# One copy of the weighting loop in the second cross attention: mask products under a condition, sums cleared first, first mask taken among the queries

## The reference, cut to what matters

```python
# first layer: keys and queries normalised per head; a padding mask over the 8192 keys
attn = jnp.where(padding_mask[:, None, None, :], attn, -jnp.inf)
# second layer
scores = jnp.einsum('bhqd,bhkd->bhqk', Q, K) / jnp.sqrt(jnp.float32(D))
scores = jnp.where(mask == 1, jnp.float32(-1000000000.0), scores)   # (1, 1, 512, 8192)
attn = jax.nn.softmax(scores, axis=-1)
out = jnp.einsum('bhqk,bhkd->bhqd', attn, V)
return out.transpose(0, 2, 1, 3).reshape(Bq, Sq, E) @ Wo.T + bo
```

## Time and profile before

| | us |
|---|---|
| median of 3 runs | 1766.46 |
| the 3 runs | 1765.86 to 1768.48 |
| the profiled execution, its own time | 1768.05 |
| its span, first to last instruction | 1766.3 |
| L0x, from the start to the end of its denominators | 0 to 463 |
| self attention and mixture of the first layer | to 985 |
| L1x, first half | 985 to 1209 |
| L1x, second half up to the inverse of the denominators | 1209 to 1411 |

### The profile page before, as it was taken

One profiled execution on the slowest core, in us unless ns is written; L12 is line 12 of the kernel. 1 busy time (PEld: TensorE's weight loads), 2 busy tenths in 40 slices (PEclk: granted clock), 3 DMA queues, 4 the chain that ended last, 5 costly groups with the idle time before them and its releaser, 6 DMA issues. The chain is left out here.

```text
span 1766.3 us, 27736 instructions
## 1 busy us (share of the span) xinstructions
PE 1614.9 (91%) x9395; PEld 738.8 (42%) x9407; DVE 1043.2 (59%) x1683; ACT 510.7 (29%) x771; POOL 101.3 (6%) x82
## 2 busy tenths in 40 slices
PE   6899998999889889999999699998989789989997
PEld 3233333222333376666665233332222134467775
DVE  5677777999745541111112589997979845743223
ACT  2434325777313310000001111113657512200000
POOL 0100001000002010000001200000200000110001
PEclk9899979999989989999999799988999999989999
DMA  4333442211056966666661313220421021229996
GB/s 161 145 136 116 162 160 80 62 49 36 0 139 111 208 245 238 236 230 231 232 229 48 126 61 113 100 85 31 156 61 48 1 83 31 97 84 335 327 324 226
DMA packets 73577, 244.67 MB, mean 139 GB/s; under 512 B 7344, under 2 KB 20544, under 8 KB 53536
## 3 DMA queue, kind: packets, MB, share of 16 engines
q1 hardware_dynamic: 64896, 224.62, 38.6%
q10 hardware_dynamic: 6048, 10.69, 1.6%
q0 software_dynamic: 2560, 8.39, 1.4%
HBM read 218.24 MB, written 35.91 MB: 144 GB/s over the span
## 5 line engine op out<-in xcount | busy, mean ns | idle before, releaser
L1489 ACT ACTIVATE BIG<-banks 128x1024 f32<-128x1024 f32 (+5 forms) x320 | 282.1, 933 | 132.1 <-PE banks L1428 132.1
L1023 DVE CUSTOM_DVE_ANT_0 BIG<-banks,MASK,MX 128x512 bf16<-128x512 f32 (+5 forms) x384 | 229.1, 655 | 64.3 <-issue 36.8
L2010 PEld LDWEIGHTS banks<-KF,BIG 128*128 128x128 f32 x1792 | 226.9, 191 | 14.1 <-issue 14.1
L2010 PE MATMUL banks<-KF,BIG 128*128 128x160 f32 (+1 forms) x1792 | 229.4, 289 | 2.4 <-DVE KF L1737 2.0
L676 PE MATMUL banks<-KF,XN 32*128 32x512 f32 (+4 forms) x1280 | 200.6, 632 | 18.2 <-DVE MX L1023 9.2
L2038 PE MATMUL banks<-BIG,PB 128*128 128x512 f32 x448 | 202.9, 600 | 0.0
L1425 PE MATMUL banks<-XN,KF 32*128 32x512 f32 (+4 forms) x1280 | 173.7, 613 | 25.9 <-issue 6.9
L1539 DVE TENSOR_TENSOR PB<-PB,BIG 128x2048 f32<-128x2048 f32 (+5 forms) x78 | 166.6, 2136 | 25.5 <-ACT BIG L1489 23.9
L1016 DVE TENSOR_REDUCE MXW<-banks 128x2 f32<-128x1024 f32 x128 | 150.3, 1216 | 52.5 <-PE banks L687 51.5
L651 PE MATMUL banks<-WV,XNT 128*128 128x512 f32 x320 | 162.0, 627 | 0.0
L1391 PE MATMUL banks<-BIG,V 128*32 128x512 f32 (+4 forms) x1280 | 158.5, 566 | 3.7 <-ACT BIG L1489 2.8
(11 more groups left out here) (284 smaller groups left out, 1411.3 us busy)
## 6 DMA issues: line engine op xcount, KB each, us to landing
BIG<-in_L0f_w SPq DMA_DIRECT2D x64, 1024.0 KB, 4.8
BIG<-in_L1f_w SPq DMA_DIRECT2D x48, 1024.0 KB, 5.6
BIG<-in_mask_q SPq DMA_DIRECT2D x16, 1024.0 KB, 9.6
CT<-in_ctx SPq DMA_DIRECT2D x9, 1024.0 KB, 4.7
XNT<-in_ctx SPq DMA_DIRECT2D x8, 1024.0 KB, 5.8
k_saved<-KF SPq DMA_DIRECT2D x32, 256.0 KB, 2.6
v_saved<-V SPq DMA_DIRECT2D x24, 256.0 KB, 2.4
KF<-k_saved SPq DMA_DIRECT2D x24, 256.0 KB, 3.4
```

The lines of the kernel that those rows point to most:

```text
L1023: last = v.tensor_tensor_reduce(m.JUNK[:, 2 * half + e, k0:k1], pair[:, e, k0:k1], bias, 1.0, mx, ALU.add, ALU.max, mx)
L1489: a.activation(m.PE_[:, s % NP, 2 * half:2 * half + 2, q0:q1], m.pair[(2 * s + half) % 3][:, :, q0:q1], ACT.Exp).then_inc(exp_ready, 1)
L2010: last = t.matmul(out, W1[k][:, d, f * P:(f + 1) * P], XE[:, d, :], start=d == 0, stop=d == DC - 1)
```

## The change

Five things, all in the code that is printed above:

- `weighted_values`, PE: the 16 steps stand once. In `scores` the products of keys and queries come first, then, under `pe.If(flag > 0)`, the four mask products, then the negated maximum. The flag of a block is read once at its start.
- the wait for the first and for the second pair of heads now stands directly ahead of the products of that pair. This holds for L0x too, which has no mask products here.
- `row_maxima`, POOL: the running sums and `OACC` are cleared at once, ahead of the wait for the list in L0x, and without the wait for the queries.
- `row_maxima`, DVE: the first block's four mask instructions (`row_bias(0)`) stand between the second and the third chunk of queries; those of later blocks stay at the start of the block, under `dve.If(i >= 1)`.
- the two self attentions take the same code as before (their waits and products are in the same order).

```diff
         def gpsimd(pool):
-            if S:
-                pool.wait_ge(S.listed, S.listed_at)
-            nb = blocks_to_do(pool, m, L)
             g = nc.gpsimd
             g.memset(m.NMX, 0.0).then_inc(slots_zeroed, 1)
...
             if not dyn:
-                return nb
+                return 1
+            for c in range(DC):
+                g.memset(m.PSUMS[c], 0.0).then_inc(zeroed, 1)
+            g.memset(m.OACC[:, :, :], 0.0).then_inc(zeroed, 1)
+            if S:
+                pool.wait_ge(S.listed, S.listed_at)
+            nb = blocks_to_do(pool, m, L)
...
-            pool.wait_ge(q_projected, DC)
-            for c in range(DC):
-                g.memset(m.PSUMS[c], 0.0).then_inc(zeroed, 1)
-            g.memset(m.OACC[:, :, :], 0.0).then_inc(zeroed, 1)
...
+            def row_bias(i):
+
+                if not isinstance(i, int):
+                    dve.wait_ge(scores_taken, first_pair(i))
+                    dve.wait_ge(mask_summed, i * NQ + B)
+                dve.wait_ge(mask_loaded, i * 16 + 16 + B)
+                for q in range(NQ):
+                    last = v.tensor_scalar(m.MB[:, q, :], m.MI[:, q, :], 1.0, m.RN[:, q:q + 1], ALU.is_equal, ALU.mult)
+                last.then_inc(bias_ready, 1)
+
             def maxima(i, ahead):
-                if dyn:
+                if L.row_mask:
+                    with dve.If(i >= 1):
+                        row_bias(i)
+                    dve.wait_ge(bias_ready, i + 1 + B)
...
                     v.scalar_tensor_tensor(QF[:, c, :], m.bank[c % 2], m.vec(L.bq)[:, c:c + 1],
                                            m.RAROWS[:, :], ALU.add, ALU.mult).then_inc(q_read, 1)
+                    if c == 1:
+                        row_bias(0)
...
-            def scores(i, s, masked):
+            def scores(i, s, flag):
...
-                for g in range(G):
+                for g in range(G if biases else 0):
                     if g % 2 == 0:
-                        pe.wait_ge(exp_ready, i * (2 * NS) + max(0, 2 * s - 2 + g // 2) + B)
+                        pe.wait_ge(exp_ready, max(0, 2 * s - 2 + g // 2))
                     for j, b in enumerate(biases):
                         t.matmul(out(g), m.IDB[:, :], b, start=j == 0, stop=False)
                 for g in range(G):
+                    if not biases and g % 2 == 0:
+                        pe.wait_ge(exp_ready, i * (2 * NS) + max(0, 2 * s - 2 + g // 2) + B)
                     t.matmul(out(g), m.KF[rows(g), c, ks], m.QF[rows(g), c, q0:q1], start=not biases, stop=False)
+                if L.row_mask:
+                    with pe.If(flag > 0):
+                        for g in range(G):
+                            t.matmul(out(g), m.IDB[:, :], m.MBK[:, kt[k], q0:q1], start=False, stop=False)
...
             def body(i):
-                if not L.row_mask:
-                    all_steps(i, False)
-                    return
-
-                flag = pe.value_load(m.CTL[0:1, bass.ds(i + C_M, 1)], min_val=0, max_val=1)
-                with pe.If(flag > 0):
-                    all_steps(i, True)
-                with pe.If(flag < 1):
-                    all_steps(i, False)
+                flag = masked(i)
+                for s in range(1, NS + 1):
+                    if s < NS:
+                        scores(i, s, flag)
+                    elif dyn:
+                        with pe.If(i + 1 < nb):
+                            scores(i + 1, 0, masked(i + 1))
+                    times_values(i, s - 1)
```

More of the change, by code:

```diff
@@ L987, in scale @@
                     v.tensor_tensor(s, s, m.pair[(2 * at + half) % 3], ALU.mult).then_inc(scores_taken, 1)
-            def maxima(i, ahead):
-                if dyn:
+            def row_bias(i):
[6 more added lines that the diff above has]
+                last.then_inc(bias_ready, 1)
+            def maxima(i, ahead):
+                if L.row_mask:
[3 more added lines that the diff above has]
+                elif dyn:
                     dve.wait_ge(scores_taken, first_pair(i))
                     dve.wait_ge(mask_loaded, i * 16 + 16 + B)
[L994 to L1000, removed]
+                    v.tensor_scalar(m.KEYROW, m.KM[:, 0:KB], m.mask_factor, m.mask_offset, ALU.mult, ALU.add).then_inc(bias_ready, 1)
                     dve.wait_ge(bias_ready, i + 1 + B)
@@ L1408, in scores @@
                 biases = []
-                if masked:
-                    biases = [m.MBK[:, kt[k], q0:q1]]
-                elif not dyn:
+                if not dyn:
                     parts = BIAS_PARTS[L.fixed] if kt[k] in (0, KT_ - 1) else 1
@@ L1430, in scores, with masked, body @@
                         last.then_inc(scores_ready, 1)
-            def first_scores(i):
+            def masked(i):
                 if not L.row_mask:
-                    scores(i, 0, False)
-                    return
-                flag = pe.value_load(m.CTL[0:1, slice(C_M, C_M + 1) if isinstance(i, int) else bass.ds(i + C_M, 1)], min_val=0, max_val=1)
-                with pe.If(flag > 0):
-                    scores(i, 0, True)
-                with pe.If(flag < 1):
-                    scores(i, 0, False)
-            def all_steps(i, masked):
+                    return None
+                return pe.value_load(m.CTL[0:1, slice(C_M, C_M + 1) if isinstance(i, int) else bass.ds(i + C_M, 1)], min_val=0, max_val=1)
+            def body(i):
+                flag = masked(i)
                 for s in range(1, NS + 1):
                     if s < NS:
-                        scores(i, s, masked)
+                        scores(i, s, flag)
                     elif dyn:
                         with pe.If(i + 1 < nb):
-                            first_scores(i + 1)
+                            scores(i + 1, 0, masked(i + 1))
                     times_values(i, s - 1)
-            def body(i):
-                if not L.row_mask:
-                    all_steps(i, False)
-                    return
-                flag = pe.value_load(m.CTL[0:1, bass.ds(i + C_M, 1)], min_val=0, max_val=1)
-                with pe.If(flag > 0):
-                    all_steps(i, True)
-                with pe.If(flag < 1):
-                    all_steps(i, False)
             M.tensor(pe, nb * KT_ + A.B, nb * NQ + A.B)
@@ L1468, in tensor @@
                 pe.wait_ge(M.flags, M.flags_at)
-            first_scores(0)
+            scores(0, 0, masked(0))
             over_blocks(pe, L, nb, body)
```

## The result

| | before | after |
|---|---|---|
| median, us | 1766.16 | 1744.84 |
| runs, us | 1764.95 to 1768.48 | 1742.83 to 1754.18 |
| span of the profiled execution, us | 1766.3 | 1741.7 |

The ratio is 0.9883, with a 95% interval of 0.986 to 0.9907. The forecast of 1744 lies within a microsecond of the median. That close a hit is partly luck: several terms of the sum were wrong and cancelled, and the profiled execution, 24.6 us shorter than the one before, has 3.5 us of gain in a part that the change doesn't touch.

What follows compares the result with a forecast made beforehand. PE, busy 91% of the span, was taken as the bound. Terms of +2.7, -1.5, -7.7, -5.15, -5.85, -5.0, -2.0 and +1.5 us took 1768.05 to 1745.0; with the median 1.6 lower, 1744 was forecast, range 1735 to 1757.

## What to carry to other kernels

A loop that holds the same code twice for a rare case pays for it the first time that each far jump is taken, here 3.3 to 3.7 us each and the slow clock behind them; a short branch in every step costs nothing where the engine has work queued. Put a rare group of products ahead of those whose wait it can cover, and put each wait directly ahead of the product that needs it, even if the engine behind is the busier one: it may lag by the depth of its buffers, and what is to be paid is its lag at the end, once. Idle time of POOL at the start of a program isn't free, since its memsets stop casts and wide TENSOR_SCALARs of DVE that everything else waits for.

## What the runs showed of the hardware

- A memset on POOL holds up DVE's cast of 128x128 (0.15 to 1.66 us), a TENSOR_SCALAR of 16x16 (0.28 to 1.04) and the four mask instructions of 128x512 (1.66 to 7.38 for four), but not a TENSOR_SCALAR of one element a partition (0.14) or a copy of one out of PSUM (0.14). What it costs depends on when they meet: 2.2 or 4.0 us at the first product.
- A branch over 256 products took 3371 ns once and 204 to 223 ns three times; over 768 products 3636 and 6371 ns, then 204 ns.
- Stages without any change differ by up to 9 us of 350 between kernels (347.6 to 356.6), with a mean granted clock of 0.97 in the shortest and 0.96 in the longest; PE was busy for 321.3 and 325.5 us of them. Differences under 4 us had to be read stage by stage.
